# Layer-norm statistics of the feed-forwards on ScalarE with running sums, in a feed-forward, attention, feed-forward kernel on one Trainium2 core

## The chip, the core and the metric

The kernel runs on one core of one Trainium2 chip. The core has five engines, each with its own in-order instruction queue: TensorE (PE, matrix products and transposes; its weight loads are listed apart as PEld), VectorE (DVE), ScalarE (ACT), GpSimd (POOL) and SyncE (SP, which only starts DMAs here). An engine whose next instruction waits for a semaphore runs nothing that stands behind it in its queue. The metric is the device time of one execution in microseconds (us).

## What is computed

The input x is 8 x 1024 rows of 256 fp32 values. Cut to what matters:

```python
def _layernorm(x, eps=1e-05):
    m = jnp.mean(x, axis=-1, keepdims=True)
    v = jnp.var(x, axis=-1, keepdims=True)
    return (x - m) / jnp.sqrt(v + eps)

def ffn(x, w_gate, w_up, w_down):      # 256 -> 704 -> 256
    # fp4_linear: both operands rounded to FP4 in blocks of 16 with a scale (max|block| / 6)
    gate, y = fp4_linear(x, w_gate), fp4_linear(x, w_up)
    return fp4_linear(jax.nn.silu(gate) * y, w_down)

x = x + 0.5 * ffn(_layernorm(x), ...)
x = x + attention(_layernorm(x), ...)  # 16 heads of 16, causal
x = x + 0.5 * ffn(_layernorm(x), ...)
```

## The kernel before, in words

x stays in SBUF for the whole kernel (`xs`), as 64 tiles of 128 rows. Three stages follow each other: the first feed-forward (`feed_forward(0, ...)`, which also prepares the weights in its first steps), the attention, and the second feed-forward (`feed_forward(1, ...)`, whose first steps carry the output projection of the attention). The change is in the two feed-forwards.

A feed-forward is a software pipeline over steps i = -6 to 63. Each engine has its own function `step(i, par)`, and the order of the lines in it is the order of the engine's queue; `steps` runs it for i = -6 to 3 as straight code, for 4 to 57 as a loop of 9 x 6 steps, and for 58 to 63 as straight code again, with `begin` and `end` hooks for the work of the neighbouring stages. One step works on several tiles at once, since a tile passes through it over some ten steps. Every hand-over between engines is a semaphore counted by tile (`done(engine, name, i)` waits until `name` has been signalled for tile i).

The parts of tile t, in the order of its dependences, with engine and line:

- statistics: DVE `bn_stats` (L712, into `ffn_stats`) and `bn_aggr` (L770, mean and variance into `ffn_aggr`), in step t-6
- POOL adds eps (L824, `ffn_eps_var`), raises to the power -1/2 (L827, `ffn_rstd`) in step t-5, and makes -mean x rstd (L786, `ffn_shift`)
- ACT writes z = x * rstd + shift (L919, `ffn_z`) in step t-5
- FP4 rounding of z: DVE maximum (L730, `ffn_amax`), POOL `ffn_dscale` (L840), DVE reciprocal `ffn_rec` (L756), POOL z/scale (L793, `v_z`, in the buffer that the trace calls q_stack), ACT magnitude (L907), DVE L741 and L762, POOL `ffn_xq` (L818); then PE transposes it (L987), ACT and DVE split it in a high and a low part (L874, L704)
- PE gate and up projection (L935) in step t, ACT `silu` (L896), DVE h = silu x up (L720)
- the same FP4 rounding of h: DVE maximum (L735), the same `ffn_dscale`, `ffn_rec` and `ffn_nscale` (L851), POOL h/scale (L857, `v_h`), ACT magnitude (L869), DVE L675 and L681, POOL `ffn_hq` (L802), PE transposes (L951), ACT high part (L880, `hT_high`), DVE low part (L665, `hT_low`)
- PE down projection (L942 to L945), DVE residual (L670)

The names of the trace: `v_h`, `v_z`, `silu` and `h` lie in memory that the attention uses for its stacks, so `q_stack` and `k_stack` stand for them in rows of these lines.

In one step, the queues between the loop's branches are: ACT silu(i), magnitude of h(i-1), magnitude of z(i+3), z(i+5), xT_high(i+2), hT_high(i-2). POOL hq(i-2), xq(i+2), eps and rstd(i+5), dscale(i), shift(i+5), v_z, nscale, v_h(i). DVE hT_low(i-3), bn_stats(i+6), h(i), maxima, u_z, u_h(i-1), residual(i-3), rec(i), g_h(i-1), g_z, xT_low(i+2), bn_aggr(i+6). The steps i = 0 to 2 (`early`) have some of these in another order.

## Time and profile before

| | us |
|---|---|
| median of 3 runs (lowest, highest) | 2045.32 (2043.16, 2047.75) |
| profiled execution, its time | 2042.67 |
| its span, first to last instruction | 2040.9 |
| PE busy | 1968.1 (96%) |
| DVE busy | 1838.1 (90%) |
| ACT busy | 1342.3 (66%) |
| POOL busy | 1089.2 (53%) |

TensorE's granted clock has the mean 0.998, which is the level of 2.4 GHz nearly throughout. The rows are from this one execution. A row of a timeline gives the start, the duration, the engine, the line, the operation and "output<-inputs"; in square brackets stands how long the engine had sat idle before it and what released it. The time of a feed-forward is read from the starts of one line that runs once a step, such as h at L720.

### The profile page before, as it was taken

The numbers are of one execution on the slowest core, as the hardware profiler recorded it, in microseconds if no ns is written. First come the engines' busy times: TensorE is split into PE (matmuls) and PEld (weight loads), VectorE is DVE, ScalarE is ACT, GpSimd is POOL, SyncE is SP. The second block draws the span as 40 slices with busy tenths as digits, with TensorE's granted clock in tenths as the row PEclk, the third lists the DMA queues.
The fourth block names the chain that finished last, engine by engine and source line by source line (L and its number), as shares of the span: only waits on it lengthen the run. The fifth ranks groups of instructions, "written<-read, shape, count | busy, mean of one in ns | idle before, by whom it ended". The sixth has DMA issues, their size and how long they took to land. (4 is left out here: it accounts for less than half of the span.)

```text
span 2040.9 us, 44249 instructions
## 1 busy us (share of the span) xinstructions
PE 1968.1 (96%) x13211; PEld 1294.5 (63%) x13211; DVE 1838.1 (90%) x4649; ACT 1342.3 (66%) x2323; POOL 1089.2 (53%) x1785
## 2 busy tenths in 40 slices
PE   4999999998999999999999999999988899999999
PEld 3788888887887333333333333333328788888888
DVE  7999999998787899999999999999937899999997
ACT  5545454544886788888888888888894354545453
POOL 5888888885664222221222222222222788888885
PEclk9999999999999999999999999999999999999999
DMA  6000000001876555455555554555335000000000
GB/s 214 17 0 0 0 0 0 0 0 45 265 235 200 133 143 141 133 138 139 139 139 148 144 134 137 135 139 140 107 104 190 6 22 16 20 21 21 15 21 26
DMA packets 134841, 185.02 MB, mean 91 GB/s; under 512 B 24928, under 2 KB 76512, under 8 KB 134368
## 3 DMA queue, kind: packets, MB, share of 16 engines
q1 hardware_dynamic: 132000, 182.11, 31.4%
q8 instruction: 73, 1.20, 0.2%
q10 hardware_dynamic: 2688, 1.05, 0.2%
q14 instruction: 80, 0.66, 0.1%
HBM read 113.90 MB, written 85.98 MB: 98 GB/s over the span
## 5 line engine op out<-in xcount | busy, mean ns | idle before, releaser
L1921 POOL TENSOR_SCALAR_AFFINE_SELECT diag_scores<-diag_scores 128x256 f32<-128x256 f32 (+1 forms) x320 | 148.3, 463 | 678.0 <-ACT diag_scores L1891 670.5
L1395 DVE CUSTOM_DVE_ANT_0 gu_ps<-gu_ps,mask_qk 128x256 f32<-128x256 f32 (+3 forms) x690 | 340.3, 528 | 51.6 <-PE gu_ps L1380 44.2
L1380 PE MATMUL gu_ps<-k_stack,q_stack 96*128 96x512 bf16 (+3 forms) x1050 | 317.3, 334 | 2.7 <-DVE part_max L1400 0.5
L1827 PE MATMUL gu_ps<-probs,v_group 128*17 128x512 f32 (+3 forms) x3072 | 310.8, 492 | 3.0 <-ACT probs L1897 1.8
L935 PE MATMUL gu_ps<-wguT_hi,ffn_xT_hi 128*128 128x512 f32 (+1 forms) x768 | 309.1, 403 | 1.2 <-DVE ffn_xT_lo L704 1.2
L919 ACT ACTIVATE ffn_z<-xs,ffn_shift,ffn_rstd 128x256 f32 (+1 forms) x128 | 76.9, 601 | 323.1 <-POOL ffn_shift L786 323.0
L935 PE MATMUL gu_ps<-wguT_hi,ffn_xT_lo 128*128 128x512 f32 (+1 forms) x768 | 287.5, 374 | 0.0
L935 PE MATMUL gu_ps<-wguT_lo,ffn_xT_hi 128*128 128x512 f32 (+1 forms) x768 | 287.3, 374 | 0.0
L1893 ACT ACTIVATE probs<-hT_ps 128x256 f32<-128x256 f32 (+2 forms) x320 | 259.7, 811 | 15.5 <-PE hT_ps L1803 15.3
L1893 ACT ACTIVATE probs<-av_ps 128x256 f32<-128x256 f32 (+2 forms) x320 | 263.6, 824 | 0.2
L1380 PEld LDWEIGHTS gu_ps<-k_stack,q_stack 96*128 96x128 bf16 x1050 | 95.4, 97 | 255.8 <-DVE part_max L1395 183.1
L1400 DVE TENSOR_REDUCE part_max<-gu_ps 128x1 f32<-128x512 f32 x360 | 235.1, 683 | 4.5 <-PE gu_ps L1380 1.4
L1803 PE MATMUL hT_ps<-q_stack,k_stack 98*128 98x512 bf16 (+3 forms) x768 | 228.1, 327 | 8.3 <-DMA v_group<-v_ones 4.2
L802 POOL TENSOR_TENSOR ffn_hq<-ffn_g_h,ffn_nscale 128x704 f32<-128x704 f32 (+1 forms) x256 | 210.5, 843 | 6.3 <-PE hT_ps L951 3.2
L942 PE MATMUL xd_ps<-wdT_hi,ffn_hT_hi 128*128 128x256 f32 x630 | 186.1, 295 | 8.9 <-DVE ffn_hT_lo L665 3.9
L1803 PE MATMUL av_ps<-q_stack,k_stack 98*128 98x512 bf16 (+3 forms) x768 | 191.3, 326 | 2.1 <-ACT probs L1893 1.9
L857 POOL TENSOR_TENSOR q_stack<-k_stack,ffn_rec 128x704 f32<-128x704 f32 x128 | 178.1, 1392 | 15.9 <-DVE ffn_rec L756 6.5
L942 PE MATMUL xd_ps<-wdT_hi,ffn_hT_lo 128*128 128x256 f32 x630 | 176.0, 279 | 0.0
L942 PE MATMUL xd_ps<-wdT_lo,ffn_hT_hi 128*128 128x256 f32 x630 | 175.7, 279 | 0.0
L1395 DVE CUSTOM_DVE_ANT_0 xd_ps<-xd_ps,mask_qk 128x128 f32<-128x128 f32 (+3 forms) x334 | 154.7, 493 | 6.1 <-PE xd_ps L1380 5.6
L935 PEld LDWEIGHTS gu_ps<-wguT_hi,ffn_xT_lo 128*128 128x128 f32 x768 | 144.1, 188 | 22.9
L935 PEld LDWEIGHTS gu_ps<-wguT_hi,ffn_xT_hi 128*128 128x128 f32 x768 | 144.6, 188 | 19.6 <-DVE ffn_xT_lo L704 1.9
(220 smaller groups left out, 4884.3 us busy)
## 6 DMA issues: line engine op xcount, KB each, us to landing
q_stack<-q_parts SPq DMA_DIRECT2D x192, 128.0 KB, 3.4
k_stack<-k_parts SPq DMA_DIRECT2D x192, 128.0 KB, 3.5
o_all<-o_sb SPq DMA_DIRECT2D x64, 256.0 KB
q_parts<-qkv_parts SPq DMA_DIRECT2D x32, 384.0 KB, 2.8
k_parts<-qkv_parts SPq DMA_DIRECT2D x32, 384.0 KB, 4.3
v_ones<-qkv_vst SPq DMA_DIRECT2D x16, 544.0 KB, 4.0
v_group<-v_ones SPq DMA_DIRECT2D x32, 272.0 KB, 4.3
xs<-in_L_attn_x SPq DMA_DIRECT2D x8, 1024.0 KB, 8.4
```

Of the source, the lines that this page charges most:

```text
L802: last = G.tensor_tensor(blocks(hq[:, to:to + n]), blocks(g_h[:, of:of + n]), spread(nscale[:, par, of // BLK:(of + n) // BLK]), ALU.mult)
L857: G.tensor_tensor(blocks(v_h[:, par, :]), blocks(h[:]), spread(rec[:, OF_H]), ALU.mult).then_inc(s["v_h"], 1)
L919: S.activation(z[:, 1 - par, :], x_tile(i + 5), ACT.Identity, bias=shift[:], scale=rstd[:]).then_inc(s["z"], 1)
L935: last = T.matmul(gu_ps[:, n, 0:cols.stop - cols.start], x[:, buf, k * P:(k + 1) * P], w[:, k, cols], start=k == 0 and m == 0, stop=k == K ...
L942: T.matmul(to, x[:, k * P:(k + 1) * P], w[:, k, :], start=k == 0 and n == 0, stop=False)
L1380: mm = T.matmul(out[:, e, :], qs[0:STACK, h0 + e, t * P:(t + 1) * P], ks[0:STACK, h0 + e, c * CHUNK:c * CHUNK + w], start=True, stop=True)
L1395: last = V.tensor_tensor_reduce(out=ps[:, e * w:(e + 1) * w], in0=ps[:, e * w:(e + 1) * w], in1=mask_qk[:, CHUNK - w:CHUNK], scale=1.0, sc ...
L1400: last = V.tensor_reduce(part_max[:, h0:h0 + per, t, c], ps[:, 0:per * w].rearrange("p (h w) -> p h w", h=per), AX.X, ALU.max)
L1803: mm = T.matmul(scores[pair][:, e, at:at + w], ks[0:STACK_MAX, h, t * P:(t + 1) * P], qs[0:STACK_MAX, h, (j + 1) * CHUNK - w:(j + 1) * CHUNK],
L1827: mm = T.matmul(o_ps[h * VPAD:h * VPAD + VCOLS, CHUNK - w:CHUNK], vs[:, t, h, :], probs[:, h // 2, i % 2, h % 2, at:at + w], start=first, ...
L1893: S.activation(probs[:, pair, i % 2, :, first:w], scores[pair][:, :, first:w], ACT.Exp, scale=DH ** -0.5).then_inc(s[pr], 1)
L1921: G.affine_select(out=block_of, in_=block_of, compare_op=ALU.is_ge, fill=MASKED, base=0, pattern=[[0, 2], [0, count], [1, P]], channel_mul ...
```

## The change

In both feed-forwards the two DVE operations go away. In their place:

- ACT reads x once with `Copy` and a running sum over the row (`total`, in step t-6, right behind z(t-1)), and POOL makes `minus_mean` = -total / 256 of it (`averaged`), as the last operation of its step t-6.
- ACT reads x a second time with `Square`, the bias `minus_mean` and a running sum (`squares`), as the first operation of its step t-5, ahead of silu. For i up to 3 it stands at the end of the step before, which is the same place in the queue save for the hooks.
- POOL's eps operation becomes squares / 256 + eps (a tensor_scalar), and its shift minus_mean x rstd (a tensor_tensor).
- The element results of both passes go to a scratch piece of memory (`q_stack` in rows) that nothing reads. The waits for the loads of x move from DVE to ACT, and ACT waits for the attention's residual in the second feed-forward's first steps.

```diff
@@ vector step
-                            if ok(i + 6):
-                                done(dve, "aggr", i + 5)
-                                V.bn_stats(stats[:], x_tile(i + 6)).then_inc(s["stats"], 1)
...
-                            if ok(i + 6):
-                                done(dve, "stats", i + 6)
-                                done(dve, "shift", i + 5)
...
-                            if ok(i + 6):
-                                V.bn_aggr(aggr[:], stats[:]).then_inc(s["aggr"], 1)
@@ gpsimd
+                            G.tensor_tensor(shift[:], minus_mean[:], rstd[:], ALU.mult).then_inc(s["shift"], 1)
+
+                        def averaged(i):
+                            done(pool, "stats", i)
+                            done(pool, "shift", i - 1)
+                            done(pool, "squares", i - 1)
+                            pool.nop(nofuse=True)
+                            G.tensor_scalar(minus_mean[:], total[:], -1.0 / DIM, 0.0, ALU.mult,
+                                            ALU.add).then_inc(s["aggr"], 1)
...
+                                done(pool, "squares", i + 5)
                                 done(pool, "z", i + 4)
+                                pool.nop(nofuse=True)
+                                G.tensor_scalar(eps_var[:], squares[:], 1.0 / DIM, EPS, ALU.mult,
                                                 ALU.add).then_inc(s["eps"], 1)
...
+                            if ok(i + 6):
+                                averaged(i + 6)
@@ scalar
+                        def squared(i):
+                            done(act, "aggr", i)
+                            done(act, "eps", i - 1)
+                            done(act, "squares", i - 1)
+                            act.nop(nofuse=True)
+                            S.activation(scratch, x_tile(i), ACT.Square, bias=minus_mean[:],
+                                         accum_out=squares[:]).then_inc(s["squares"], 1)
+
+                        def at_once(i):
+
+                            return isinstance(i, int) and i <= 2
+
                         def step(i, par):
+                            if ok(i + 5) and not at_once(i - 1):
+                                squared(i + 5)
...
                                 S.activation(z[:, 1 - par, :], x_tile(i + 5), ACT.Identity, bias=shift[:],
                                              scale=rstd[:]).then_inc(s["z"], 1)
+                            if ok(i + 6):
+
+                                done(act, "aggr", i + 5)
+                                act.nop(nofuse=True)
+                                S.activation(scratch, x_tile(i + 6), ACT.Copy,
+                                             accum_out=total[:]).then_inc(s["stats"], 1)
...
+                            if ok(i + 6) and at_once(i):
+                                squared(i + 6)
```

ACT's queue over one step of the loop. Before, from hT_high of one step (L880) to hT_high of the next:

```order
L880 CAST ffn_hT_hi<-hT_ps 128x768 [waits ffn_hT,ffn_hT_lo,ffn_down]
L896 ACTIVATE k_stack<-gu_ps 128x704 [waits ffn_gate,ffn_h]
L869 ACTIVATE av_ps<-q_stack 128x704 [waits ffn_v_h,ffn_g_h,ffn_g_z]
L907 ACTIVATE av_ps<-q_stack 128x256 [waits ffn_v_z,ffn_g_z,ffn_g_h]
...
L919 ACTIVATE ffn_z<-xs,ffn_shift,ffn_rstd 128x256
L874 CAST ffn_xT_hi<-xd_ps 128x256 [waits ffn_xT,ffn_up]
```

The same stretch after the change. Its lines carry new numbers: hT_high L878, silu L908, the magnitudes L867 and L919, z L932, xT_high L872:

```order
L878 CAST ffn_hT_hi<-hT_ps 128x768 [waits ffn_hT,ffn_hT_lo,ffn_down]
L635 REGISTER_ALU
L891 ACTIVATE q_stack,ffn_squares<-xs,ffn_minus_mean 128x256 [waits ffn_squares,ffn_aggr,ffn_eps]
L908 ACTIVATE k_stack<-gu_ps 128x704 [waits ffn_gate,ffn_h]
L867 ACTIVATE av_ps<-q_stack 128x704 [waits ffn_v_h,ffn_g_h,ffn_g_z]
L919 ACTIVATE av_ps<-q_stack 128x256 [waits ffn_v_z,ffn_g_z,ffn_g_h]
L932 ACTIVATE ffn_z<-xs,ffn_shift,ffn_rstd 128x256 [waits ffn_v_z,ffn_shift]
L938 ISA [waits ffn_aggr]
L938 ACTIVATE q_stack,ffn_total<-xs 128x256
L872 CAST ffn_xT_hi<-xd_ps 128x256 [waits ffn_xT,ffn_up]
```

The pass for the squares (L891) stands between hT_high and silu and waits for `ffn_aggr`, which POOL now signals; the pass for the sum (L938) stands between z and xT_high.

POOL's queue at the end of a step of the loop, where that signal comes from. Before, from dscale on, into the next step's `ffn_hq`:

```order
L840 TENSOR_SCALAR ffn_dscale<-ffn_amax 128x60 [waits ffn_rec,ffn_amax_z,ffn_amax_h]
L786 TENSOR_SCALAR ffn_shift<-ffn_aggr,ffn_rstd 128x1 [waits ffn_rstd]
L793 TENSOR_TENSOR q_stack<-ffn_z,ffn_rec 128x256 [waits ffn_rec,ffn_u_z]
L851 TENSOR_SCALAR ffn_nscale<-ffn_amax 128x60 [waits ffn_hq,ffn_xq]
L857 TENSOR_TENSOR q_stack<-k_stack,ffn_rec 128x704 [waits ffn_rec,ffn_u_h]
L802 TENSOR_TENSOR ffn_hq<-ffn_g_h,ffn_nscale 128x704 [waits ffn_g_h,ffn_hT]
```

After, with dscale at L836, shift L774, v_z L788, nscale L847, v_h L853 and hq L797:

```order
L836 TENSOR_SCALAR ffn_dscale<-ffn_amax 128x60 [waits ffn_rec,ffn_amax_z,ffn_amax_h]
L774 TENSOR_TENSOR ffn_shift<-ffn_minus_mean,ffn_rstd 128x1 [waits ffn_rstd]
L788 TENSOR_TENSOR q_stack<-ffn_z,ffn_rec 128x256 [waits ffn_rec,ffn_u_z]
L847 TENSOR_SCALAR ffn_nscale<-ffn_amax 128x60 [waits ffn_hq,ffn_xq]
L853 TENSOR_TENSOR q_stack<-k_stack,ffn_rec 128x704 [waits ffn_rec,ffn_u_h]
L635 REGISTER_ALU
L781 TENSOR_SCALAR ffn_minus_mean<-ffn_total 128x1 [waits ffn_squares,ffn_stats,ffn_shift]
L797 TENSOR_TENSOR ffn_hq<-ffn_g_h,ffn_nscale 128x704 [waits ffn_g_h,ffn_hT]
```

`ffn_minus_mean` (L781, which signals `ffn_aggr`) stands behind v_h (L853) of the step. Before, that signal came from DVE's `bn_aggr`.

## Rows read from the trace of the kernel before

**Rows 1.** Busy time in two stretches of the two feed-forwards (us, instructions).
```profile
core 0: us, PE busy (x) PEld busy (x) DVE busy (x) ACT busy (x) POOL busy (x), PEclk, DMA share, GB/s
100.00:200.00 100.00, 100.00 (x636) 89.30 (x635) 98.26 (x190) 50.08 (x87) 88.57 (x148) 1.00 0.00 0
...
1650.00:1750.00 100.00, 100.00 (x629) 88.79 (x628) 97.97 (x192) 51.34 (x88) 87.57 (x148) 1.00 0.06 21
```

**Rows 2.** Waits from 60 to 440 us: total us, times, longest us.
```profile
ACT ffn_z L919 <- POOL ffn_shift L786: 152.0, 55, 2.8
...
ACT av_ps L869 <- POOL q_stack L857: 21.0, 56, 2.9
...
PEld xd_ps L942 <- issue: 10.8, 46, 2.7
```

**Rows 3.** ACT's timeline from 436 to 450 us.
```profile
438.78 0.60 ACT L919 ACTIVATE ffn_z<-xs,ffn_shift,ffn_rstd 128x256 f32 x1 [2.78 <-POOL ffn_shift L786]
439.38 0.37 ACT L874 CAST ffn_xT_hi<-xd_ps 128x256 fp32r<-128x256 f32 x1
439.65 0.81 ACT L880 CAST ffn_hT_hi<-hT_ps 128x768 fp32r<-128x768 f32 x1
441.05 0.76 ACT L896 ACTIVATE k_stack<-gu_ps 128x704 f32<-128x704 f32 x1 [0.59 <-PE gu_ps L935]
...
445.56 0.60 ACT L919 ACTIVATE ffn_z<-xs,ffn_shift,ffn_rstd 128x256 f32<-128x256 f32 x1 [2.74 <-POOL ffn_shift L786]
...
447.58 0.76 ACT L896 ACTIVATE k_stack<-gu_ps 128x704 f32<-128x704 f32 x1 [0.31 <-PE gu_ps L935]
```

**Rows 4.** POOL's timeline in the same stretch.
```profile
445.20 0.26 POOL L786 TENSOR_SCALAR ffn_shift<-ffn_aggr,ffn_rstd 128x1 f32<-128x1 f32 x1
445.89 0.62 POOL L793 TENSOR_TENSOR q_stack<-ffn_z,ffn_rec 128x256 f32<-128x256 f32 x1 [0.43 <-DVE ffn_rec L756]
...
447.10 1.39 POOL L857 TENSOR_TENSOR q_stack<-k_stack,ffn_rec 128x704 f32<-128x704 f32 x1
```

**Rows 5.** DVE's timeline in the same stretch.
```profile
440.23 0.17 DVE L770 BATCH_NORM_AGGREGATE ffn_aggr<-ffn_stats 128x2 f32<-128x6 f32 x1
440.49 0.96 DVE L665 TENSOR_TENSOR ffn_hT_lo<-hT_ps,ffn_hT_hi 128x768 fp32r<-128x768 f32 x1
441.84 0.89 DVE L720 TENSOR_TENSOR k_stack<-k_stack,gu_ps 128x704 f32<-128x704 f32 x1 [0.39 <-ACT k_stack L896]
...
445.23 0.52 DVE L756 RECIPROCAL ffn_rec<-ffn_dscale 128x60 f32<-128x60 f32 x1
...
448.62 0.89 DVE L720 TENSOR_TENSOR k_stack<-k_stack,gu_ps 128x704 f32<-128x704 f32 x1 [0.36 <-PE gu_ps L935]
```

**Rows 6.** Groups of instructions by line, 60 to 440 us: busy, mean ns, idle before.
```profile
L712 DVE BATCH_NORM_STATS2 ffn_stats<-xs 128x6 f32 (+1 forms) x55 | 23.0, 417 | 0.0
...
L770 DVE BATCH_NORM_AGGREGATE ffn_aggr<-ffn_stats 128x2 f32<-128x6 f32 x55 | 9.4, 171 | 0.0
...
L907 ACT ACTIVATE av_ps<-q_stack 128x256 fp32r<-128x256 f32 x56 | 20.8, 371 | 1.2 <-DVE ffn_g_h L681 1.2
...
L786 POOL TENSOR_SCALAR ffn_shift<-ffn_aggr,ffn_rstd 128x1 f32<-128x1 f32 x56 | 14.8, 265 | 5.4 <-POOL ffn_rstd L827 0.2
L824 POOL TENSOR_TENSOR ffn_eps_var<-ffn_aggr,eps_tile 128x1 f32<-128x1 f32 x56 | 10.6, 190 | 0.0
```

**Rows 7.** DVE's timeline: h of tile 0 (first feed-forward), tiles 0 and 58 (second).
```profile
44.56 0.87 DVE L720 TENSOR_TENSOR k_stack<-k_stack,gu_ps 128x704 f32<-128x704 f32 x1
...
1594.83 0.87 DVE L720 TENSOR_TENSOR k_stack<-k_stack,gu_ps 128x704 f32<-128x704 f32 x1
...
1989.13 0.89 DVE L720 TENSOR_TENSOR k_stack<-k_stack,gu_ps 128x704 f32<-128x704 f32 x1 [0.37 <-PE gu_ps L935]
```

**Rows 8.** ACT's timeline in the first steps of the second feed-forward.
```profile
1587.73 0.37 ACT L874 CAST ffn_xT_hi<-xd_ps 128x256 fp32r<-128x256 f32 x1 [7.23 <-PE xd_ps L987]
...
1592.88 0.60 ACT L919 ACTIVATE ffn_z<-xs,ffn_shift,ffn_rstd 128x256 f32<-128x256 f32 x1 [2.90 <-POOL ffn_shift L786]
```

More of the change, by code:

```diff
@@ L542, in scalar @@
                     S.activation(next_table[:, :], minus_half[:, :], ACT.Silu)
+                out_done(act, "resid", 2 if part < OUT_PARTS - 1 else OUT_CHUNKS - 1)
             def gpsimd(pool, part):
@@ L569, in output_projection @@
             return {"sync": sync, "tensor": tensor, "scalar": scalar, "vector": vector, "gpsimd": gpsimd}
-        names = ("stats aggr eps rstd shift z amax_z amax_h dscale nscale rec v_h v_z av_h av_z u_h u_z g_h g_z hq xq "
+        names = ("stats aggr squares eps rstd shift z amax_z amax_h dscale nscale rec v_h v_z av_h av_z u_h u_z g_h g_z hq xq "
                  "xT xT_hi xT_lo gate up silu h hT hT_hi hT_lo down resid stored").split()
@@ L590, in feed_forward @@
                 OF_H, OF_Z = slice(0, NB_H), slice(NB_H, NB)
-                stats, aggr, eps_var, rstd, shift = (tmp("stats", [P, 6]), tmp("aggr", [P, 2]), tmp("eps_var", [P, 1]),
-                                                     tmp("rstd", [P, 1]), tmp("shift", [P, 1]))
+                total, minus_mean, squares, eps_var, rstd, shift = (
+                    tmp(n, [P, 1]) for n in ("total", "minus_mean", "squares", "eps_var", "rstd", "shift"))
                 xq = tmp("xq", [P, DIM])
@@ L763, in step @@
                                                        op0=ALU.max, op1=ALU.subtract).then_inc(s["g_z"], 1)
[L764 to L766 removed]
                             if ok(i + 2) and not (early(i, -2) and i == -2):
                                 xT_low(i + 2, par)
[L769 to L779 removed]
+                        steps("vector", dve, step, finish)
                     @block.gpsimd
@@ L785, in shifted @@
                             pool.nop(nofuse=True)
-                            G.tensor_scalar(shift[:], aggr[:, 0:1], rstd[:], -1.0, ALU.mult,
-                                            ALU.mult).then_inc(s["shift"], 1)
+                            G.tensor_tensor(shift[:], minus_mean[:], rstd[:], ALU.mult).then_inc(s["shift"], 1)
[6 more added lines that the diff above has]
+                                            ALU.add).then_inc(s["aggr"], 1)
                         def over_scale_z(i, par):
@@ L925, in step, with other_batches @@
                                 hT_high(i - 2)
-                        steps("scalar", act, step, finish)
+                            if ok(i + 6) and at_once(i):
+                                squared(i + 6)
+                        def other_batches(i):
+                            if i is None:
+                                for b in range(2, BATCH):
+                                    act.wait_ge(x_loaded[b], 16)
+                            elif (i + AHEAD) % SEQ_TILES == 0:
+                                act.wait_ge(x_loaded[(i + AHEAD) // SEQ_TILES], 16)
+                        steps("scalar", act, step, finish, other_batches if phase == 0 else None)
                     @block.tensor
```

11 lines of the change are left out of this document (2 added, 9 removed).

## The prediction

> **What bounds the kernel now.** I read three views: busy time by stretch, the waits, and the timelines of one step on ACT, POOL and DVE side by side. In both feed-forwards PE is busy for all of a 100 us stretch, DVE for 98, POOL for 88 and ACT for 50 [rows 1]. So the step is a near tie of PE and DVE, with POOL not far off, and only ACT has room. Its length comes from the starts of h: in the first feed-forward h of tile 0 starts at 44.56 [rows 7] and h of tile 58 at 441.84 [rows 5], that is 397.3 us for 58 steps; in the second 1989.13 - 1594.83 = 394.3 us for 58 steps [rows 7]. The mean is 6.82 us a step, and in the steady part it is nearer 6.80 (441.84 to 448.62 is 6.78) [rows 5]. The waits say where ACT's room is: 152.0 us in 55 steps, 2.8 us each, ahead of z, for shift from POOL [rows 2]. PE's only wait that recurs is 10.8 us in 46 times ahead of the down projection, 0.23 us each [rows 2].
>
> By the totals the change looks right, since it takes work from the engine at 98% and gives it to the one at 50%. What decides is where the new work stands in the queues, and what it waits for.
>
> **Part 1, DVE loses two operations a step.** bn_stats is 417 ns and bn_aggr 171 ns [rows 6], together 0.59 us a step. Both were in the queue between hT_low and h or ahead of hT_low; none of the later DVE operations changes. If DVE were the only bound, a step could fall to 6.2 us. PE however is full: without its recurring wait of 0.23 us it needs 6.80 - 0.23 = 6.57 us a step. So this part alone is worth at most 0.23 us a step, 27 us in the 116 steps.
>
> **Part 2, ACT gains two passes over 128 x 256.** The rows have no ACTIVATE with a running sum, so the price has to be bounded. The lower end is the magnitude of z, 371 ns with no operand per row [rows 6], which a successor overlaps a little: some 0.30 us from start to start. The nearest row is z itself, which reads the same tile, writes to SBUF and takes two per-row operands: 0.60 us, and its successor starts 0.60 us after it (438.78 to 439.38) [rows 3]. I take 0.55 us for the pass of squares, nearer to z since the pass also has a per-row operand and an SBUF output, and since the sum has to be written. The upper end is a sum that costs an operation of its own, 0.60 + 0.35 = 0.95 us. Two passes are about 1.0 us a step. ACT has some 3.4 us idle in a step [rows 1], so by volume they are hidden.
>
> The Trainium skill prices this too (ScalarE: Activation LUTs, "What ACT_TABLE_LOAD costs"): 186 ns + 0.833 ns per column with immediate scale and bias, 93 ns more per per-row operand, and some 93 ns of overlap between neighbours. That makes z 585 ns where the trace has 602, and the magnitude 399 where it has 371; a Square with one such operand would be an estimated 0.49 us, 0.40 us from start to start. With that figure the sum below would come out 17 us lower, at 2228. It says nothing of what the running sum costs, and no row here does.
>
> **Part 3, the order, which is the large term.** The squares of a tile need its mean, and the mean now comes from POOL. POOL makes `minus_mean` as the last operation of its step, behind v_h. ACT makes the squares as the first operation of its next step, ahead of silu. Now put the two timelines on one clock. ACT ends hT_high at 439.65 + 0.81 = 440.46 and would take up the squares there; it starts silu of tile 58 at 441.05 and of tile 59 at 447.58 [rows 3]. POOL works on v_h of tile 58 from 447.10 to 448.49 [rows 4]. So in the kernel before, silu of the next tile starts 0.91 us ahead of the end of v_h. After the change it can't: silu(i+1) is queued behind the squares, these wait for minus_mean, and that stands behind v_h(i) in POOL's queue. silu is followed by the same tile's h, and h leads through rec to the next v_h. The steps are thus tied in one ring that admits no overlap. Its parts, each from a row:
>
> - h start to rec start on DVE: 441.84 to 445.23 = 3.39 us [rows 5]. Between them stand five operations of DVE's queue (two maxima, u_z, u_h, residual), none of which the change touches.
> - rec start to end of v_h on POOL: 445.23 [rows 5] to 448.49 [rows 4] = 3.26 us. It holds rec 0.52, 0.14 to POOL, v_z, nscale and v_h. Nothing in it changes.
> - minus_mean: 0.09 us to start it (v_z ends at 446.51 and nscale, also a tensor_scalar, begins at 446.60) [rows 4] and 0.265 us, the price of shift, a tensor_scalar of 128 x 1 [rows 6]: 0.36 us.
> - POOL to ACT: shift ends at 445.46 [rows 4], z starts at 445.56 [rows 3], 0.10; in the loop a register operation and a nop stand ahead, so 0.13 us.
> - the squares, to silu's start: 0.55 us (0.30 to 0.95).
> - silu start to h start: 441.05 [rows 3] to 441.84 [rows 5] = 0.79 us, a place where h did wait for silu.
>
> Sum: 3.39 + 3.26 + 0.36 + 0.13 + 0.55 + 0.79 = 8.48 us. Since every other chain of a step fits into less (PE 6.57 us, DVE 6.2, POOL 0.88 x 6.8 = 6.0 plus 0.36), the step becomes 8.48 us. PE then waits where it had been full. The ring holds for the steps in which the squares of a tile are made ahead of a silu that needs an earlier v_h: 58 steps in each feed-forward, 116. 116 x 8.48 = 983.7 us against 397.3 + 394.3 = 791.6: **+192 us**. From tile 59 on no statistics are left and the old pace returns.
>
> **Part 4, small edits.** eps becomes a tensor_scalar (190 to about 265 ns) and shift a tensor_tensor (265 to about 190) [rows 6]: nothing together, and both are off the ring, covered by POOL's wait for rec (0.43 us) [rows 4]; without that cover they would still cancel. The pass for the sum stands ahead of xT_high and hT_high and delays hT_low by 0.55 us less the 0.26 us that bn_aggr frees ahead of it (440.23 to 440.49) [rows 5]. In a step of 8.48 us that lies inside the time in which ACT waits for minus_mean; in a step of 6.8 us it would cost (a rival below). ACT's added waits for x and for the residual are those that DVE had, and PE's last one is the same. The functions are all covered by the table that is loaded: three table loads stand in ACT's queue before and after.
>
> **Part 5, the first steps.** In steps -6 to -1 the path of a tile's statistics now goes ACT, POOL, ACT, 0.37 + 0.13 + 0.36 + 0.13 + 0.49 = 1.5 us, and ACT's work for the weights or the projection queues behind it. If nothing hides it: 12 x 1.5 = 18 us, and steps 0 to 2 have v_z between v_h and minus_mean, some 0.6 us x 6 = 3.5 us. If all hides, 0: in the second feed-forward ACT idles 7.23 and 2.90 us there [rows 8]. I take 10 of 0 to 22.
>
> **Sum.** The profiled execution took 2042.67 us (span 2040.9), 2.65 us under the median of the three runs, so either base is the same within the noise. 2042.67 + 192 + 10 = **2245 us**.
>
> **Rivals.**
>
> A: *the running sum is dear.* Each pass carries an operation of its own behind it, and the squares take 0.95 us from start to start or more. Nothing in the rows excludes it. The ring becomes 8.9 to 9.1 us: 116 x 0.5 = 58 us more, about 2303 us.
>
> B: *the ring does not close, only the passes cost.* If minus_mean were there when ACT comes to it, the passes would still stand on ACT's way to hT_low and h: silu 0.55 us later against a slack of 0.3 to 0.4 us, hT_low 0.3 us later, PE's down projection with it. 0.3 to 0.8 us in 116 steps is 35 to 93 us; about 2105 us. It needs minus_mean by about 440.46, and POOL's v_h of the step before, which minus_mean has to follow, ends later than silu's start; the order of the queues speaks against it.
>
> C: *faster, because DVE is freed.* The same condition, and the passes must fit in ACT's idle time: then PE's 0.23 us a step go, up to 27 us: 2016 to 2042, with about 2029 in the middle. The point from which it decides is the same: minus_mean ready before ACT has ended hT_high. In the trace v_h ends 0.91 us after the next silu had already started, and minus_mean comes after that. I see nothing that would move v_h ahead by this much, since rec, on which it waits, is set by DVE's five operations, which stay.
>
> **How the numbers follow.** The ring as priced 0.78, A 0.14, B 0.05, C 0.03. The ring's own range: with the squares at 0.30 and the other hops 0.02 us shorter, 8.20 us and no cost in the first steps: 116 x 8.20 - 791.6 = 160, 2203 us. With the squares at 0.8, 8.73 and 20 us in the first steps: 221 + 20, 2284. To leave out no more than 2 in 10 the range goes on to the middle of A: 2203 to 2305. About 0.2% is what a measurement of this kernel can tell from no change. Only C is faster, 0.03, and a corner of it is within 0.2%: faster 0.03, same 0.01, slower 0.96.
>
> **What would show it.** In the changed kernel's waits a new line must lead on ACT: the pass of squares (L891) released by POOL's `ffn_minus_mean` (L781), near 110 times. The starts of h must stand 8.5 us apart. PE's busy share in a stretch such as 200 to 300 us should fall to about 6.6 / 8.5, 78%, with waits for DVE's h or hT_low, DVE's to 6.1 / 8.5, 72%, and DVE should now wait for silu. The step of 8.48 is wrong if the squares' row differs from 0.55 us; the ring is wrong if L891 starts at once behind hT_high. I would be wrong as a whole if h still starts every 6.8 us.

## The result, and the profile after

| | before | after |
|---|---|---|
| median of the runs | 2044.24 us (2042.7 to 2047.75, 4 runs) | 2229.59 us (2228.61 to 2231.14, 4 runs) |
| ratio, 95% interval | | 1.0909 (1.0895 to 1.0922) |
| span of the profiled execution | 2040.9 us | 2229.3 us |
| h of tile 0 / tile 58, first feed-forward | 44.56 / 441.84 | 52.78 / 539.86 |
| h of tile 0 / tile 58, second | 1594.83 / 1989.13 | 1694.61 / 2177.72 |

The change costs 185 us; 2245 had been predicted, 2203 to 2305 as the range. The starts of h, from DVE's timeline of the changed kernel (start, duration, engine and line, operation, and in brackets the idle time ahead of it with what ended it):

```profile
52.78 0.89 DVE L720 TENSOR_TENSOR k_stack<-k_stack,gu_ps 128x704 f32<-128x704 f32 x1 [1.05 <-ACT k_stack L908]
...
539.86 0.89 DVE L720 TENSOR_TENSOR k_stack<-k_stack,gu_ps 128x704 f32<-128x704 f32 x1 [2.15 <-ACT k_stack L908]
...
1694.61 0.89 DVE L720 TENSOR_TENSOR k_stack<-k_stack,gu_ps 128x704 f32<-128x704 f32 x1 [1.11 <-ACT k_stack L908]
...
2177.72 0.89 DVE L720 TENSOR_TENSOR k_stack<-k_stack,gu_ps 128x704 f32<-128x704 f32 x1 [2.08 <-ACT k_stack L908]
```

They place the whole loss. The 116 steps take 487.1 + 483.1 = 970.2 us, where they took 791.6 [rows 5, 7]: +178.6. The first steps of the first feed-forward, up to h of tile 0, take 8.2 us more. The way from tile 58 to the next feed-forward's tile 0 takes 1154.75 us against 1152.99, 1.8 more, and what follows the last tile 58 has 51.6 us against 51.8. The sum is 188.4, the difference of the spans. Beside it are the waits of the changed kernel from 60 to 440 us (total us, times, longest):

```profile
DVE k_stack L720 <- ACT k_stack L908: 98.9, 45, 3.2
ACT q_stack L891 <- POOL ffn_minus_mean L781: 87.8, 45, 4.0
ACT ffn_z L932 <- issue: 87.7, 43, 2.2
...
PE xd_ps L1015 <- DVE xs L673: 45.9, 43, 1.9
```

The second line is the one that had been named ahead: the squares wait 1.95 us a step for POOL's `minus_mean`. The first is its consequence, DVE's h waiting 2.2 us for silu, and the last its consequence for PE, which had hardly waited for anything [rows 2]. Now the three queues on one clock, as [rows 3 to 5] were for before. DVE's timeline:

```profile
205.61 0.89 DVE L720 TENSOR_TENSOR k_stack<-k_stack,gu_ps 128x704 f32<-128x704 f32 x1 [2.13 <-ACT k_stack L908]
...
208.99 0.52 DVE L756 RECIPROCAL ffn_rec<-ffn_dscale 128x60 f32<-128x60 f32 x1
...
213.93 0.89 DVE L720 TENSOR_TENSOR k_stack<-k_stack,gu_ps 128x704 f32<-128x704 f32 x1 [2.13 <-ACT k_stack L908]
```

POOL's timeline:

```profile
209.65 0.62 POOL L788 TENSOR_TENSOR q_stack<-ffn_z,ffn_rec 128x256 f32<-128x256 f32 x1 [1.20 <-DVE ffn_rec L756]
...
210.86 1.39 POOL L853 TENSOR_TENSOR q_stack<-k_stack,ffn_rec 128x704 f32<-128x704 f32 x1
212.34 0.19 POOL L781 TENSOR_SCALAR ffn_minus_mean<-ffn_total 128x1 f32<-128x1 f32 x1
```

And ACT's:

```profile
209.05 0.40 ACT L938 ACTIVATE q_stack<-xs 128x256 bf16 x1
209.36 0.19 ACT L938 ACTIVATION_READ_ACCUMULATOR q_stack<-xs 128x1 f32 x1
...
210.00 0.81 ACT L878 CAST ffn_hT_hi<-hT_ps 128x768 fp32r<-128x768 f32 x1
212.64 0.51 ACT L891 ACTIVATE q_stack<-xs,ffn_minus_mean 128x256 bf16 x1 [1.84 <-POOL ffn_minus_mean L781]
213.06 0.19 ACT L891 ACTIVATION_READ_ACCUMULATOR q_stack<-xs,ffn_minus_mean 128x1 f32 x1
213.15 0.74 ACT L908 ACTIVATE k_stack<-gu_ps 128x704 f32<-128x704 f32 x1
```

Follow one turn: h at 205.61, rec at 208.99, v_h until 212.25, `minus_mean` at 212.34, squares at 212.64, silu at 213.15, h at 213.93. That is 8.32 us. ACT ends hT_high at 210.81 and would be free for silu. In the kernel before it waited there for PE, 15.3 us in 53 times between 60 and 440 us, which is 0.29 us a step (the 0.59 of [rows 3] is step 58, the first without statistics); now the squares stand ahead of it and hold it for 2.34 us. The mean step is a little longer, since every sixth has a loop branch in it and takes some 8.56. In the second feed-forward an ordinary turn takes 8.26 us; the last section says which hand-over is shorter there.

### The profile page after: what moved, and what is told of

Its sections match the earlier page's. It is cut to its first block and busy times, and to the rows that moved or that the text cites. A ratio compares the mean times of both kernels' runs of the same rounds, so it can differ in the third digit from the quotient of the medians.

```text
span 2229.3 us, 45165 instructions
## 1 busy us (share of the span) xinstructions
PE 2027.7 (91%) x13211; PEld 1301.3 (58%) x13211; DVE 1776.1 (80%) x4393; ACT 1447.6 (65%) x2835; POOL 1110.3 (50%) x1913
## 5 line engine op out<-in xcount | busy, mean ns | idle before, releaser
L720 DVE TENSOR_TENSOR k_stack<-k_stack,gu_ps 128x704 f32<-128x704 f32 x128 | 113.7, 888 | 257.4 <-ACT k_stack L908 252.2
L932 ACT ACTIVATE ffn_z<-xs,ffn_shift,ffn_rstd 128x256 f32 (+1 forms) x128 | 76.8, 600 | 238.8 <-issue 234.9
L797 POOL TENSOR_TENSOR ffn_hq<-ffn_g_h,ffn_nscale 128x704 f32<-128x704 f32 (+1 forms) x256 | 210.7, 844 | 11.5 <-DVE ffn_g_h L684 8.2
L891 ACT ACTIVATE q_stack<-xs,ffn_minus_mean 128x256 bf16 (+1 forms) x128 | 65.4, 511 | 231.5 <-POOL ffn_minus_mean L781 231.4
L853 POOL TENSOR_TENSOR q_stack<-k_stack,ffn_rec 128x704 f32<-128x704 f32 x128 | 178.2, 1392 | 15.8 <-DVE ffn_rec L756 6.4
```

The source lines that it names most:

```text
L720: V.tensor_tensor(h[:], silu[:], up_ps, ALU.mult).then_inc(s["h"], 1)
L797: last = G.tensor_tensor(blocks(hq[:, to:to + n]), blocks(g_h[:, of:of + n]), spread(nscale[:, par, of // BLK:(of + n) // BLK]), ALU.mult)
L853: G.tensor_tensor(blocks(v_h[:, par, :]), blocks(h[:]), spread(rec[:, OF_H]), ALU.mult).then_inc(s["v_h"], 1)
```

## Experiments

The theory: *a ring.* h, rec, v_h, minus_mean, squares, silu and the next h admit no overlap. The rivals: the volume of the two passes on ACT; the pass for the sum in front of hT_high; and, once the ring is open, the question what else holds the step, DVE, POOL's own queue or PE. Steps are given as first / second feed-forward in the steady part: 6.81 / 6.81 before, 8.36 / 8.31 after, as means with the longer sixth steps in them.

**mean_ahead: one link moved on POOL.** After, with `minus_mean` ahead of v_h instead of behind it:

```diff
+                            if ok(i + 6):
+                                averaged(i + 6)
                             if ok(i):
                                 done(pool, "u_h", i - 2)
...
-                            if ok(i + 6):
-                                averaged(i + 6)
```

> The changed kernel with one edit: POOL makes minus_mean ahead of v_h instead of behind it. All work is the same. Ring theory: v_h (1.39 us) leaves the ring, which is then 3.38 (h to rec) + 1.79 (rec to end of nscale) + 0.39 (minus_mean and its hand-over) + 0.51 (squares) + 0.78 (silu to h) = 6.85 us; h also waits for the previous v_h, 3.38 + 1.79 + 0.28 + 1.39 + 0.13 = 6.97 us. So a step near 6.97 us in place of 8.37, 116 x 1.40 = 162 us less: about 2067 us (2058 to 2080). Rival, that the two passes cost by their volume on ACT: no change, about 2230 us.

Measured: 2077.93 us, 1.0173 (1.0154 to 1.0191), step 7.07 / 7.01. Of the 185 us 152 are gone, with two lines in another place. ACT's squares now start without a wait in the steady part (no bracket on L891 in its timeline). The step that had been expected is 6.97 us; what sets it at 7.07 is POOL's own ring, described under late_squares.

**late_squares: the other link, moved on ACT.** After, with the squares behind the magnitude of z, in ACT's gap ahead of z:

```diff
                         def step(i, par):
-                            if ok(i + 5) and not at_once(i - 1):
-                                squared(i + 5)
...
+                            if ok(i + 5) and not at_once(i - 1):
+                                squared(i + 5)
                             if ok(i + 5):
                                 done(act, "v_z", i + 3)
```

> The changed kernel with one edit: from step 4 on, ACT makes the squares between the magnitude of z and z, no longer ahead of silu. Ring theory: nothing that silu needs stands behind v_h any more, the longest remaining rings are about 6 us, and the step is PE's and DVE's, 6.6 to 6.8 us: 2035 to 2060 us, the upper end if the step is 6.8 and the 10 us of the first steps stay. Rival (volume of the passes): about 2230 us. Second rival, that the pass for the sum ahead of xT_high and hT_high costs too: 0.3 us a step, 35 us more, about 2090 us.

Measured: 2098.12 us, 1.0261 (1.0244 to 1.0278), step 7.19 / 7.13. The ring is open again, but the time missed what had been expected: something holds the step at 7.19. POOL's timeline shows it:

```profile
300.69 0.62 POOL L788 TENSOR_TENSOR q_stack<-ffn_z,ffn_rec 128x256 f32<-128x256 f32 x1 [0.43 <-DVE ffn_rec L756]
301.40 0.42 POOL L847 TENSOR_SCALAR ffn_nscale<-ffn_amax 128x60 f32<-128x60 f32 x1
301.90 1.39 POOL L853 TENSOR_TENSOR q_stack<-k_stack,ffn_rec 128x704 f32<-128x704 f32 x1
303.38 0.19 POOL L781 TENSOR_SCALAR ffn_minus_mean<-ffn_total 128x1 f32<-128x1 f32 x1
303.53 1.64 POOL L797 TENSOR_TENSOR ffn_hq<-ffn_g_h,ffn_nscale 128x704 f32<-128x704 f32 x2
...
306.76 0.42 POOL L836 TENSOR_SCALAR ffn_dscale<-ffn_amax 128x60 f32<-128x60 f32 x1
...
307.88 0.62 POOL L788 TENSOR_TENSOR q_stack<-ffn_z,ffn_rec 128x256 f32<-128x256 f32 x1 [0.43 <-DVE ffn_rec L756]
```

and DVE's, where rec now waits for POOL:

```profile
307.21 0.53 DVE L756 RECIPROCAL ffn_rec<-ffn_dscale 128x60 f32<-128x60 f32 x1 [0.35 <-POOL ffn_dscale L836]
```

POOL's wait of 0.43 us looks like room, and isn't. v_z waits for rec, rec for dscale, and dscale stands at the end of POOL's own queue, behind the last v_z. From v_z to the end of dscale POOL works 307.18 - 300.69 = 6.49 us without a pause, and the way over DVE takes 0.70: 7.19. rec begins 0.03 to 0.04 us after dscale's end in every step of two stretches of the feed-forwards (100 to 420 us and 1700 to 1950), so POOL's ring sets the step throughout. The same ring in the kernel before, POOL's timeline:

```profile
200.73 0.62 POOL L793 TENSOR_TENSOR q_stack<-ffn_z,ffn_rec 128x256 f32<-128x256 f32 x1 [0.48 <-DVE ffn_rec L756]
...
201.94 1.39 POOL L857 TENSOR_TENSOR q_stack<-k_stack,ffn_rec 128x704 f32<-128x704 f32 x1
203.29 1.65 POOL L802 TENSOR_TENSOR ffn_hq<-ffn_g_h,ffn_nscale 128x704 f32<-128x704 f32 x2
...
206.38 0.42 POOL L840 TENSOR_SCALAR ffn_dscale<-ffn_amax 128x60 f32<-128x60 f32 x1
...
207.51 0.62 POOL L793 TENSOR_TENSOR q_stack<-ffn_z,ffn_rec 128x256 f32<-128x256 f32 x1 [0.36 <-DVE ffn_rec L756]
```

6.07 us and 0.71 over DVE: 6.78 in a step of 6.81. So POOL had next to no room before either, at a busy share of 88%. How much it had can be read from rec, which begins 0.07 us after dscale's end in the mean of the first feed-forward and 0.15 in the second, where 0.03 is the least: 0.04 and 0.11 us of room. The change adds to that queue: from v_h's start to hq's it is 1.63 us, where it was 1.35 (minus_mean, +0.28), and eps, now behind a nop, begins 0.71 us after xq where it was 0.58 (+0.13). (act_mean, below, has the wait for the squares ahead of eps but no nop, and its way from v_z to the end of dscale is 6.08 us, so it is not the wait that costs this.) In mean_ahead, where minus_mean falls between nscale and v_h, it costs 0.15 instead of 0.28, which makes 6.78 + 0.13 + 0.15 = 7.06, against 7.07 measured.

**both_in_gap.** late_squares, with the pass for the sum behind the squares too, so that nothing new stands ahead of hT_high:

```diff
+                            if ok(i + 6) and not at_once(i - 1):
+                                done(act, "aggr", i + 5)
+                                act.nop(nofuse=True)
+                                S.activation(scratch_2, x_tile(i + 6), ACT.Copy,
+                                             accum_out=total[:]).then_inc(s["stats"], 1)
...
-                            if ok(i + 6):
+                            if ok(i + 6) and at_once(i - 1):
```

> As late_squares, and from step 4 on the pass for the sum stands there too, behind the squares and ahead of z, where ACT waited 2.8 us for shift in the kernel before. Ring theory: 2030 to 2058 us; if the sum's place ahead of hT_high cost anything in late_squares, this one is faster by that. Volume: about 2230 us.

Measured: 2098.49 us, 1.0259 (1.0242 to 1.0276). It is late_squares to 0.4 us, a miss by the same cause: the place of the sum's pass costs nothing, POOL's ring sets the step.

**passes_alone: the volume by itself.** Before, with the two passes at the places that they have in after; nobody reads their sums, and DVE keeps its statistics. A nop ahead of z comes with them, which the lines below leave out.

```diff
                         def step(i, par):
+                            if ok(i + 5):
+                                done(act, "spare", i + 4)
+                                act.nop(nofuse=True)
+                                S.activation(scratch, x_tile(i + 5), ACT.Square, bias=minus_half[:, 0:1],
+                                             accum_out=spare_squares[:]).then_inc(s["spare"], 1)
...
+                            if ok(i + 6):
+                                done(act, "stats", i + 6)
+                                done(act, "spare_2", i + 5)
+                                act.nop(nofuse=True)
+                                S.activation(scratch_2, x_tile(i + 6), ACT.Copy,
+                                             accum_out=spare_total[:]).then_inc(s["spare_2"], 1)
```

> The kernel before, VectorE's statistics kept, with two ScalarE passes of the same size and with running sums in the places where the change has them; nobody uses their results and they wait for nothing on POOL (the bias of the Square pass is a constant). Ring theory: the passes' volume is free, because the longest way through ACT is 6.35 us in a step of 6.8: 2044 to 2060 us. Volume theory: 0.93 us a step, 108 us more, 2150 us or above.

Measured: 2058.28 us, 1.0065 (1.0048 to 1.0081), step 6.92 / 6.90. The passes as such, at these places and beside DVE's statistics, cost 14 of the 185 us. About 0.07 of the 0.1 us a step appears in PE's timeline as a longer pause ahead of the down projection, from the last matmul of the up projection to the first of it: 0.30 us in the mean from 200 to 400 us, where the kernel before has 0.22. Where the rest arises isn't shown.

**squares_twice and total_twice: a pass on the ring, and one beside it.** After, with the pass of squares run twice:

```diff
+                            S.activation(scratch_2, x_tile(i), ACT.Square, bias=minus_mean[:],
+                                         accum_out=spare_sum[:]).then_inc(s["spare"], 1)
+                            act.nop(nofuse=True)
                             S.activation(scratch, x_tile(i), ACT.Square, bias=minus_mean[:],
```

> The changed kernel; the pass of squares is run twice in a row in its place, the first into spare memory. Ring theory: this pass is a link of the ring, so each copy counts in full, its measured 0.51 us from start to silu's start: 116 x 0.51 = 59 us more, 2289 us (2280 to 2295). A theory in which only the lateness of minus_mean costs, with ACT idle otherwise, gives less.

and with the pass for the sum twice:

```diff
+                                S.activation(scratch_2, x_tile(i + 6), ACT.Copy,
+                                             accum_out=spare_sum[:]).then_inc(s["spare"], 1)
                                 S.activation(scratch, x_tile(i + 6), ACT.Copy,
```

> The changed kernel; the pass for the sum is run twice in a row in its place between z and xT_high. The same added work on the same engine as in squares_twice. Ring theory: it is not a link of the ring and ACT waits 1.8 us for minus_mean behind it, so nothing: 2230 us (2227 to 2238). Volume theory: 0.4 us a step, 50 us more, 2280 us.

Measured: squares_twice 2291.32 us, 1.1203 (1.1184 to 1.1222), +62, step 8.84 / 8.78; total_twice 2233.17 us, 1.0919 (1.09 to 1.0937), +4, step 8.37 / 8.29. Two passes of nearly the same size, 0.51 and 0.40 us; one costs 62 us, and the other 4, which its interval doesn't tell from the 1.0909 of after and which aren't in the step. ACT's timeline of squares_twice shows the second pass full in silu's way, 0.49 us from start to start; the step grows by 0.48 us, 56 us in 116 steps, and the other 5 or 6 lie ahead of and between them:

```profile
303.94 0.51 ACT L893 ACTIVATE k_stack<-xs,ffn_minus_mean 128x256 bf16 x1 [1.99 <-POOL ffn_minus_mean L783]
304.36 0.19 ACT L893 ACTIVATION_READ_ACCUMULATOR k_stack<-xs,ffn_minus_mean 128x1 f32 x1
304.45 0.49 ACT L896 ACTIVATE q_stack<-xs,ffn_minus_mean 128x256 bf16 x1
304.85 0.19 ACT L896 ACTIVATION_READ_ACCUMULATOR q_stack<-xs,ffn_minus_mean 128x1 f32 x1
304.94 0.74 ACT L913 ACTIVATE k_stack<-gu_ps 128x704 f32<-128x704 f32 x1
```

In ACT's timeline of total_twice most of the second pass, some 0.28 of its 0.40 us, falls in the pause that xT_high had ahead of it: 0.19 us of idle time, and 0.09 us by which xT_high now overlaps the sum's read. The rest comes off the wait for minus_mean, 1.75 us where it was 1.84. The turn stays, 8.32 us from 300.00 to 308.32:

```profile
300.00 0.51 ACT L893 ACTIVATE q_stack<-xs,ffn_minus_mean 128x256 bf16 x1 [1.67 <-POOL ffn_minus_mean L783]
...
308.32 0.51 ACT L893 ACTIVATE q_stack<-xs,ffn_minus_mean 128x256 bf16 x1 [1.75 <-POOL ffn_minus_mean L783]
```

With these the ring is shown from both sides: opening it at either of two links takes most of the loss away, and lengthening it is paid in full (0.48 us for a pass of 0.49). What remained was whether the idea can gain anything at all.

**no_statistics: its upper bound.** Before, with bn_stats and bn_aggr left out.

```diff
-                            if ok(i + 6):
-                                done(dve, "aggr", i + 5)
-                                V.bn_stats(stats[:], x_tile(i + 6)).then_inc(s["stats"], 1)
...
-                            if ok(i + 6):
-                                V.bn_aggr(aggr[:], stats[:]).then_inc(s["aggr"], 1)
+                        V.memset(aggr[:], 1.0).then_inc(s["aggr"], 1)
```

> The kernel before without VectorE's bn_stats and bn_aggr and with nothing in their place: mean 1 and variance 1 are set once, so the statistics are left out of the computation. This gives what VectorE's relief alone is worth. If VectorE were the bound: a step of 6.57 us (TensorE's own), 2015 us. Second theory, from late_squares: POOL's own queue forms a ring with rec, from v_z to the end of dscale 6.07 us and 0.70 us through rec back to v_z, 6.77 us: then the relief is worth 0.04 us a step, and the time is 2030 to 2042 us, most of the gain from the first steps.

Measured: 2042.95 us, 0.9988 (0.9974 to 1.0001), step 6.81 / 6.82. Taking 0.59 us a step from the engine that is busy 98% of the time gives nothing that can be told from zero.

**act_mean and act_mean_nscale: nothing new on POOL.** ACT makes the mean by itself (the pass for the sum scales by -1/4096, so that its running sum is -mean/16, and the squares take scale 1/16), and both passes stand in gaps. The second kernel also moves nscale from POOL to DVE.

```diff
-                        def averaged(i):
-                            done(pool, "stats", i)
...
+                            S.activation(scratch_2, x_tile(i), ACT.Copy, scale=-1.0 / (16 * DIM),
+                                         accum_out=minus_mean[:]).then_inc(s["aggr"], 1)
...
+                                V.tensor_scalar(nscale[:, par, of], amax[:, of], -1.0 / 6.0, -SCALE_MIN,
+                                                ALU.mult, ALU.min).then_inc(s["nscale"], 1)
...
-                                G.tensor_scalar(nscale[:, par, of], amax[:, of], -1.0 / 6.0, -SCALE_MIN,
-                                                ALU.mult, ALU.min).then_inc(s["nscale"], 1)
```

> The two passes on ScalarE with no operation of POOL between them: the first pass scales by -1/4096, so that its running sum is -mean/16 and serves as the bias of the second, which scales by 1/16 and sums up to the variance. eps and shift on POOL are the operations of the kernel before. From step 4 on the first pass stands behind silu and the second behind the magnitude of z. POOL-ring theory: POOL's queue is that of the kernel before, so the step is 6.77 to 6.80 us: 2035 to 2055 us with the first steps. Volume theory: 2230 us. If VectorE's relief paid in full: 2015 us.

> act_mean with one more edit: nscale (a tensor_scalar of 128 x 60, 0.42 us on POOL and 0.50 us with its gap) is made by VectorE, in the time that bn_stats and bn_aggr left free, ahead of the residual. POOL-ring theory: POOL's ring falls from 6.77 to 6.27 us, VectorE's queue is at 6.2 + 0.2 = 6.4 us, and the step becomes TensorE's, 6.57 to 6.70 us: 2015 to 2035 us. If POOL's ring is not what holds act_mean, its time does not change.

Measured: act_mean 2048.71 us, 1.0021 (1.0011 to 1.0031), step 6.82 / 6.83, with h of tile 0 at 48.16, 3.6 us later than before; act_mean_nscale 2048.24 us, 1.0024 (1.0014 to 1.0034), step 6.82 / 6.83. So the statistics can go to ACT at nearly no cost, but for no gain. And POOL's way from v_z to the end of dscale, 5.65 us in the second kernel where it is 6.08 in the first, wasn't alone in holding the step, which that expectation had missed.

**before_nscale.** Before, with the same move of nscale alone.

> The kernel before with the same edit alone: nscale on VectorE, statistics on VectorE as well. POOL's ring falls to 6.27 us, but VectorE, at 6.7 us busy of 6.8, gets some 0.2 us more: a step of 6.9 to 7.0 us, 2055 to 2070 us. If it is faster than the kernel before, VectorE had room and the relief of POOL alone is what pays.

Measured: 2043.84 us, 1.0003 (0.9993 to 1.0013), step 6.82 / 6.82. A loss had been expected for DVE at 98%; nscale costs it only 0.18 us, 0.10 from start to start, and the step doesn't grow by it. So DVE had at least 0.10 us of room in the kernel before.

**before_fewer and nscale_fewer: less for PE.** before and act_mean_nscale, with two of the 17 matmuls of the down projection left out, 0.24 us a step:

```diff
                                 for n, (x, w) in enumerate(passes(of, wdT)):
+                                    if n == 1 and k < 2:
+                                        continue
                                     T.matmul(to, x[:, k * P:(k + 1) * P], w[:, k, :], start=k == 0 and n == 0, stop=False)
```

> The kernel before with two of the 17 matmuls of each down projection left out (the low part of the weights times the high part of h, for the first two blocks of 128 rows; a part of the computation is left out). On TensorE this is 2 x 0.118 us = 0.24 us a step. If TensorE alone bounds the kernel before: 128 x 0.24 = 30 us less, 2014 us. If POOL's ring (6.77 us) and VectorE's queue (6.7 us) stand right behind it: 0.04 to 0.1 us a step, 2031 to 2041 us.

> act_mean_nscale with the same two matmuls left out. There POOL's ring is 6.27 us and VectorE's queue about 6.4 us. TensorE theory: it is TensorE's own queue that kept that kernel at 6.82 us, so the 0.24 us come off in full: a step of 6.58 us, 28 us less than act_mean_nscale, about 2020 us. If something else held it, its time stays at 2048 us.

Measured: before_fewer 2029.78 us, 0.9945 (0.9925 to 0.9965), step 6.79 / 6.73; nscale_fewer 2027.94 us, 0.9921 (0.9904 to 0.9938), step 6.70 / 6.69. The first is just under its expected 2031 to 2041; the second lies between what had been expected if PE alone held act_mean_nscale (2020) and if something else did (2048). The busy times from 220 to 420 us of the four kernels in question, first no_statistics (us, busy time and instructions of each engine):

```profile
220.00:420.00 200.00, 200.00 (x1262) 178.16 (x1261) 184.31 (x325) 100.50 (x177) 176.46 (x295) 1.00 0.00 0
```

act_mean_nscale:

```profile
220.00:420.00 200.00, 200.00 (x1260) 177.91 (x1259) 186.31 (x353) 126.96 (x296) 165.05 (x264) 1.00 0.00 0
```

before_nscale:

```profile
220.00:420.00 200.00, 200.00 (x1263) 177.55 (x1263) 198.12 (x411) 100.09 (x177) 163.15 (x265) 1.00 0.00 0
```

nscale_fewer:

```profile
220.00:420.00 200.00, 200.00 (x1228) 172.23 (x1227) 188.37 (x358) 128.59 (x300) 167.23 (x270) 1.00 0.00 0
```

DVE can have 184 or 198 of 200 us and POOL 163 or 176, and the step is 6.82 in the first three. Only less work for PE moves it, by 12 to 15 hundredths of the 24 where DVE and POOL both have room (20 us against act_mean_nscale), and by two hundredths in the first feed-forward and nine in the second in before_fewer. So PE holds the kernel before, with POOL's ring close behind. Its timeline shows nearly no pause:

```profile
202.82 0.34 PE L935 MATMUL gu_ps<-wguT_lo,ffn_xT_hi 128*128 128x384 f32 x1
202.99 0.34 PE L935 MATMUL gu_ps<-wguT_hi,ffn_xT_lo 128*128 128x384 f32 x1
203.22 0.36 PE L942 MATMUL xd_ps<-wdT_hi,ffn_hT_hi 128*128 128x256 f32 x1
```

The first start follows the one before it as closely as the matmuls of this size do, 0.17 us; the down projection comes 0.23 us after the last of them. In the mean this is 0.22 us from 200 to 400 us and 0.20 from 1700 to 1900, and no other place in the step is looser. So PE waits 0.05 and 0.03 us a step, and its own need is an estimated 6.76 to 6.79 us, from steps of 6.81 and 6.82.

before_fewer then stops at POOL's ring. POOL's and DVE's timelines of its second feed-forward:

```profile
1810.68 0.42 POOL L840 TENSOR_SCALAR ffn_dscale<-ffn_amax 128x60 f32<-128x60 f32 x1
1811.15 0.52 DVE L756 RECIPROCAL ffn_rec<-ffn_dscale 128x60 f32<-128x60 f32 x1
1811.74 0.63 POOL L793 TENSOR_TENSOR q_stack<-ffn_z,ffn_rec 128x256 f32<-128x256 f32 x1 [0.28 <-DVE ffn_rec L756]
```

rec begins 0.03 to 0.05 us after dscale's end in every step from 100 to 420 us and from 1700 to 1950, and the ring is 6.08 + 0.71 = 6.79 us in the first feed-forward and 6.08 + 0.65 = 6.73 in the second, which are its steps. Only about 6 of its 14 us lie in the steady steps; 8 lie between the last h of the first feed-forward and the first of the second, and no run shows their cause.

nscale_fewer is held by a third ring, which its timelines of DVE and PE show:

```profile
301.58 0.89 DVE L721 TENSOR_TENSOR k_stack<-k_stack,gu_ps 128x704 f32<-128x704 f32 x1 [0.37 <-PE gu_ps L962]
...
304.73 0.42 DVE L674 SCALAR_TENSOR_TENSOR xs<-xd_ps,xs 128x256 f32 x1
305.28 0.43 PE L1016 MATMUL xd_ps<-ident,ffn_xq 128*128 128x128 f32 x2
...
308.25 0.89 DVE L721 TENSOR_TENSOR k_stack<-k_stack,gu_ps 128x704 f32<-128x704 f32 x1 [0.37 <-PE gu_ps L962]
```

PE's transposes of xq wait for DVE's residual (`done(pe, "resid", i - 4)` stands ahead of them), the rest of the up projection stands behind them in PE's queue, h waits for it, and the next residual stands behind h in DVE's. From h to the end of the residual it is 3.57 us, to the transposes 0.13, to the next h 2.99 in the mean: 6.69, the step. The 0.13 us are 0.12 to 0.14 in every step from 200 to 400 us and from 1700 to 1900, which marks a wait; xq was ready 2 us before. In the kernel before 0.41 us lie between the two, so this ring has 0.28 us of room there. Its h to residual is 0.10 us shorter, since nscale isn't in DVE's queue. No run shortened this ring, so for nscale_fewer the cause is read from the trace and not shown by an experiment.

So in the kernel before PE needs 6.76 to 6.79 us, POOL's ring 6.78 in the first feed-forward and 6.71 in the second, and DVE has at least 0.10 us of room. No version that moved the statistics beats the kernel before; the two that are faster leave work out.

## Why the prediction was right, and where it was off

**The ring, and with it the sign and most of the size: right.** Its terms, as predicted and as the turn from 205.61 to 213.93 has them:

| term | predicted | measured |
|---|---|---|
| h to rec | 3.39 | 208.99 - 205.61 = 3.38 |
| rec to end of v_h | 3.26 | 210.86 + 1.39 - 208.99 = 3.26 |
| minus_mean | 0.36 | 0.09 + 0.19 = 0.28 |
| POOL to ACT | 0.13 | 212.64 - 212.53 = 0.11 |
| squares to silu | 0.55 | 213.15 - 212.64 = 0.51 |
| silu to h | 0.79 | 213.93 - 213.15 = 0.78 |
| step | 8.48 | 8.32 |

The ring was right and its length 0.16 us too long. The mis-sized terms are the small ones of Part 3 that no row had shown. The largest is `minus_mean`, 0.08 us: I gave it shift's price, but shift has a per-row operand (0.265 us) and minus_mean only immediates, 0.19. The mean of all 116 steps is 970.2 / 116 = 8.36 us, which is 0.12 under 8.48: 13 of the 15 us by which the time was overestimated. The longer sixth steps, which Part 3 didn't have, offset a quarter of the error in the ring; that is luck.

**Part 5**, 10 us for the first steps: 8.2 in the first feed-forward and at most 1.8 in the second, 10.0. The sum is met; that it would lie nearly all in the first feed-forward had not been said. As 10 had been taken out of a range of 0 to 22, that it is met is luck.

**Part 2 and rival A.** A had said that the running sum carries an operation of its own. It does, and still A's time isn't reached: the operation lasts 0.19 us but begins 0.09 before the pass ends, so that the squares take 0.42 + 0.09 us from start to start and not 0.95. The Trainium skill's price (ScalarE: Activation LUTs, "What ACT_TABLE_LOAD costs"), an estimated 0.49 us for the squares and 0.40 for the sum's pass without a per-row operand, stands beside rows of 0.51 and 0.40 us. The 0.09 us for the sum are in no figure of it, and with them its 0.40 from start to start becomes 0.49, against 0.51 measured. The sum by that figure, 2228, is nearer to the 2229.59 measured than 2245 is, but by luck: it has the squares 0.11 us too short, where the other terms of the ring are together 0.12 us too long.

**Part 1: right in its conclusion, wrong in its figure.** I took PE's wait line of 0.23 us [rows 2] off the step and got 6.57 us as PE's own need. But that row is of the weight load, and most of that idle time is covered by the matmuls before it: PE's matmuls wait only 0.03 to 0.05 us a step there, as their starts show. Its own need is 6.76 to 6.79 us, so the gain of up to 27 us that Part 1 and rival C spoke of did not exist (0.05 us a step would be 6). no_statistics has 0.9988 (0.9974 to 1.0001) where C would have had 2029 / 2044 = 0.993.

**"POOL 0.88 x 6.8 = 6.0 plus 0.36" among the chains that fit: wrong.** It took the busy share as POOL's need. Its queue is a ring of its own over DVE, 6.78 us before (6.71 in the second feed-forward) and 7.19 (7.13) with the change's additions, as late_squares showed. It is harmless in after, since 8.32 covers it, and is the next limit as soon as the ring is opened. Part 4 had the same error in small: it priced eps and shift by their durations, which do cancel, and called POOL's wait for rec a cover, but the nop ahead of eps adds 0.13 us to a queue without room.

**Rival B** named 2105 us for an open ring, and late_squares has 2098. That is a coincidence. B's cause was ACT's passes on the way to hT_low and h. passes_alone prices them at 14 us, in part on that very way, and both_in_gap takes the sum's pass off that way for nothing.

**What would show it.** The wait named in advance stands where it had been put, 127 times where near 110 had been said. PE's waits were to be for h or hT_low; the longest, 45.9 us, is for DVE's residual (`xs`), which stands behind h in DVE's queue. DVE's share from 200 to 300 us was 74% for 72 predicted, but PE's 87% for 78:

```profile
200.00:300.00 100.00, 86.63 (x516) 72.18 (x516) 74.14 (x133) 51.35 (x120) 73.84 (x132) 1.00 0.00 0
```

6.8 instead of 6.57 us of work makes 82. The rest is that a matmul's row before a pause is longer than its share in a close row of them: in PE's timeline eight matmuls of 128x256 start 0.12 us apart, each with a duration of 0.28, so each pause is shown 0.16 us too short. With two pauses a step, ahead of the two groups of transposes, that is 0.32 / 8.36, an estimated 4%.

## What to carry to other kernels

Before moving work to an idle engine, write down for each new value who makes it last in its queue and who reads it first in its own; if the reader stands ahead of what the maker waits for, the queues close into a ring, and its length is the step, whatever the busy shares say. An engine with a short recurring wait is not one with room: follow what ends the wait, and if that leads back into the engine's own queue, the wait is part of its step. And before work is taken from the busiest engine, leave it out altogether once; here that run says that the most the idea could gain is nothing.

## What the runs showed of the hardware

- A pass with a running sum issues a second instruction, ACTIVATION_READ_ACCUMULATOR, of 0.19 us, that adds 0.09 us from start to start. The groups by line of the changed kernel, ACT and POOL, 60 to 440 us (busy, mean ns, idle before):

```profile
L891 ACT ACTIVATION_READ_ACCUMULATOR q_stack<-xs,ffn_minus_mean 128x1 f32 x46 | 8.6, 188 | 0.0
...
L781 POOL TENSOR_SCALAR ffn_minus_mean<-ffn_total 128x1 f32<-128x1 f32 x46 | 8.8, 192 | 4.4 <-ACT q_stack L938 0.6
```

- A tensor_scalar of 128 x 1 on POOL is 192 ns with immediates and 265 with a per-row operand [rows 6]. What it costs the queue depends on its place. In late_squares v_h ends at 303.29, minus_mean with its nop ahead begins at 303.38, and hq at 303.53, 0.04 before minus_mean ends. In the kernel before, hq began 0.04 us ahead of v_h's end. The gap, the operation less the overlap at its end, and the overlap that is lost make 0.09 + 0.19 - 0.04 + 0.04 = 0.28 us. Behind nscale, where a gap of 0.08 us had been already, it is 0.15.
- nscale, 128 x 60, takes 0.42 us on POOL and 0.18 on DVE, where it adds 0.10 from start to start: from DVE's groups of before_nscale, 60 to 440 us:

```profile
L755 DVE TENSOR_SCALAR ffn_nscale<-ffn_amax 128x60 f32<-128x60 f32 x55 | 10.1, 184 | 0.0
```
- rec's start on DVE to v_z's start on POOL takes 0.66 to 0.67 us in the first feed-forward and 0.60 to 0.61 in the second, as the median of each kernel here. Above, late_squares has 307.88 - 307.21 = 0.67 and before_fewer 1811.74 - 1811.15 = 0.59. This is why each ring with this hand-over in it is some 0.06 us shorter in the second feed-forward: 8.32 and 8.26, 7.19 and 7.13, 6.79 and 6.73. What makes it shorter there no run shows.
